# Expert products of layer 0 with tokens on partitions, gated results summed into the residual

## The chip, the cores and the metric

One core of a Trainium2 chip runs the whole program in one launch. The metric is device microseconds of one execution, as the median of several runs; lower is better. The engines are PE (TensorE: matmuls and, beside them, weight loads), DVE (VectorE), ACT (ScalarE), POOL (GpSimd) and SP (SyncE, which here only issues DMAs). They run at their own pace and wait for each other by semaphores.

## The reference, cut to what matters

Two transformer layers over 4096 tokens (16 blocks of 256) of 128 features. The change touches the end of layer 0's attention part and layer 0's expert part:

```
x  = x0
x1 = x + attn(LN(x)) @ w_out + b_out
m  = gelu(LN2(x1) @ w1 + b1) @ w2 + b2                  # 128 -> 512 -> 128
xa = layernorm(x + (x1 + m))
logits = xa @ gate_weight.T                             # [4096, 8]
kth    = sort(all logits)[4*128*6 - 1]
gates  = logits * (logits >= kth)
y_e    = gelu_tanh(xa @ w1_e.T + b1_e) @ w2_e.T + b2_e  # for each of 8 experts
x      = layernorm(xa + sum_e gates[:, e] * y_e)
```

All tokens go through all eight experts (dense). Layer 1, attention and routed experts, follows and is not changed.

## The kernel before, in words

The program runs three stages one after the other: `attention_0` (layer 0's attention), `dense_0` (the m product and the experts of layer 0) and `attention_1` with the routed experts of layer 1. Nothing of one stage overlaps the next: a block ends with all engines.

**attention_0** works on 16 blocks of 256 tokens, pipelined over six stages by a table written by hand (PARTS_0, L150): each engine runs through the same list of parts and does its own share of each. POOL does in "norm" the sum `xs = x + b_out` (L306 to L309), in "stats" the power of -0.5 of the variances, and in "weights" the causal mask (L316). DVE does in "output" `x1 = product + xs` and `xs = x1 + x` (L456, L458). Small inputs come in at the start on ACT's DMA queue (L324); several engines wait for all six of them.

**dense_0** takes chunks of 512 tokens. A *job* is one chunk through one hidden layer: 8 M jobs (the m product, s = 0 to 7) and then 64 pairs (chunk, expert), chunk by chunk. JOBS is 72. All engines run a loop over steps s, and a step does the parts of several jobs, in the order in which they are written in each engine's function:

- PE: `hidden(s+2)`, the up product: 4 blocks of 128 hidden units, each 3 matmuls of 512 tokens (L1045 to L1047). Values and weights are split into a high and a low f16 half, hence three. Then the transposes for M jobs, `down(s)` (L1060), the gate logits, and one small matmul of the search. `down` has the weights stationary and the hidden values moving: 12 matmuls of 512 columns, so its result YB has features on partitions and tokens along the row. YB has two banks.
- ACT: `hidden`: the gelu of each block (L808) and the f16 high half (L813).
- DVE: `low`: the f16 low half (L867), in two passes a job.

After an **M job** ACT evicts YB to accm with scale and bias (L828), PE transposes accm back to tokens on partitions (L1091), DVE adds the residual xs (L982, "post"), does the statistics (L986, L990), POOL the power (L781, L782), and DVE the normalization into xa (L1021). PE turns xa (L1098) for the logits and the pairs. In steps 4 to 11 DVE also makes the low half of one expert's weights (L1030).

**The search** for the kth logit runs on DVE and PE in steps 10 to 27 (COUNT_0 = 10): 15 rounds with three candidates each. Then the gates are known: PE transposes them, DVE copies them to gT (L962), SP stores them to DRAM and broadcasts, for each pair, one gate row of 512 tokens over 128 partitions into the ring G of 6 (L757 to L765).

**Folding.** Until step FOLD_0 = 31 gates are missing, so the results of the first 22 pairs are kept raw: DVE adds the bias and copies YB into buffers that are free by then (L968; x1, xs, hn, h2, stage). From step 31 on each step folds the pair that has just ended (L924: (YB + b2) * G into tmp, L935: acc += tmp), and in 22 of the steps 31 to 68 one kept pair too (L921, L935). When a chunk has all eight experts, PE transposes acc (`turned_sum`, L1078), and the same post adds xa, normalizes and writes xa. Chunks end in steps 41, 44, 49, 57, 59, 65, 69 and 73. In step CLOSING = 69 DVE's order differs, to end early.

Of the kernel before, what the change touches and what calls it, by code (L numbers as in the profile page):

```python
# [87 lines left out]
class Mem:  # L88
# [33 lines left out]
    "d32": (F32, (("b1", ((E + 1) * FB,)), ("cols", (4,)), ("b2", (E,)), ("bitf", (15,)), ("bits", (45,)))),  # L122
# [51 lines left out]
def attention_0(nc, d, keep, rows, stages):  # L174
# [3 lines left out]
    with ExitStack() as ctx:  # L178
# [7 lines left out]
        bo = m.sb("bo", [P, P])  # L186
# [37 lines left out]
        xb_done = m.sem("xb_done")  # L224
# [26 lines left out]
        LOADS, CLEARS = 6, 5  # L251
# [30 lines left out]
        def _(pool):  # L282
# [19 lines left out]
            def step(what, n, k):  # L302
                if what == "stats" and n:
                    power(n)
                if what == "norm":
# [3 lines left out]
                    ins.then_inc(xb_done, 1)  # L309
                if what == "weights":  # L310
# [63 lines left out]
        def _(dve):  # L374
# [3 lines left out]
            def step(what, n, k):  # L378
# [204 lines left out]
COUNT_0 = M_JOBS + 2  # L583
ROUNDS = 15
FOLD_0 = COUNT_0 + ROUNDS + 6
G_RING = 6
LEAD = 2
BEGIN, END = -LEAD - 3, JOBS + 3
CLOSING = JOBS - 1 - LEAD


def job(s):

    return ("m", s, 0) if s < M_JOBS else ("e", (s - M_JOBS) // E, (s - M_JOBS) % E)


def is_pair(s):
    return M_JOBS <= s < JOBS


def kept_raw(s):
    return is_pair(s) and s + 1 < FOLD_0


def raw_pair(s):

    for j in range(M_JOBS, FOLD_0):
        if kept_raw(j) and FOLD_0 + (j - M_JOBS) * 9 // 5 == s:
            return j
    return None  # L610


def folds_0():

    out = []
    for s in range(FOLD_0, JOBS + 1):
        out += [(s, s - 1)]
        if raw_pair(s) is not None:
            out += [(s, raw_pair(s))]
    return out  # L620


def places_0():

    order = [j for _, j in folds_0()]
    chunk = lambda j: job(j)[1]
    place = {j: k for k, j in enumerate(order)}
    opens = {j for k, j in enumerate(order) if all(chunk(i) != chunk(j) for i in order[:k])}
    closes = {j: s for k, (s, j) in enumerate(folds_0()) if all(chunk(i) != chunk(j) for i in order[k + 1:])}
    ended = {s + 1: chunk(j) for j, s in closes.items()}  # L630
    return place, opens, set(closes), ended


def uses_0(ended):

    left, right = [], []
    for s in range(BEGIN, END):
        if 0 <= s - 1 < M_JOBS:
            left.append(("post", s - 1))
        if s in ended:  # L640
            left.append(("epost", ended[s]))
        if 0 <= s - 2 < M_JOBS:
            right.append(("turn", s - 2))
            left.append(("logits", s - 2))
# [1662 lines left out]
def layout(a):  # L2307
# [51 lines left out]
    for t in range(4):  # L2359
        b2[t, :, t] = a["L1_ffn_b2"]  # L2360
# [21 lines left out]
```

## Time and profile before

| | |
|---|---|
| median of 3 runs | 1062.15 us (1059.59, 1062.15, 1066.69) |
| span of the profiled execution, first to last instruction | 1062.5 us |
| attention_0 | 0 to 244 us |
| dense_0: M jobs; pairs | 244 to 350 us; 350 to 691 us |
| attention_1 and routed experts | 692 to 1062 us |
| PE, DVE, ACT, POOL busy | 944.1, 859.6, 756.3, 405.7 us |

The profiled execution has no time of its own beside its span, which stands 0.35 us above the median. How to read rows: engines' times are in us from the first instruction; a line number such as L924 is that of the kernel. In the order of time a row is: start, length, engine, line, operation, written tile <- read tiles, shape, count, and in brackets how long the engine sat idle before it and what ended that. PEld are weight loads, SPq and ACTq the queues that issue DMAs. Matmuls are pipelined, so the length of one is longer than the distance from one start to the next, and the distance counts.

### The profile page before, as it was taken

Reading aid. Unit: us, or ns where it says so; the run is one execution under the profiler, and the core shown is the slowest. Engines: PE = TensorE matmul, PEld = TensorE weight load, DVE = VectorE, ACT = ScalarE, POOL = GpSimd, SP = SyncE. Lnnn points to the kernel's source line nnn. Section 1 sums busy time; section 2 is a strip of 40 time slices with the busy share of each in tenths; the row PEclk is TensorE's granted clock in tenths of the full one; section 3 lists DMA queues with packets and bytes.
Section 4 is the critical chain, followed back from the end, with each engine's and each line's share of the span. In section 5 each row is a group of like instructions: output and inputs, shape, how many; then the busy total and the mean of one; then the engine's idle time right before and its main releaser. Section 6 shows DMA issues by size and latency. Waiting matters only on the chain. (4 is left out here: it accounts for less than half of the span.)

```text
span 1062.5 us, 28952 instructions
## 1 busy us (share of the span) xinstructions
PE 944.1 (89%) x10222; PEld 607.5 (57%) x10222; DVE 859.6 (81%) x2328; ACT 756.3 (71%) x1476; POOL 405.7 (38%) x568
## 2 busy tenths in 40 slices
PE   5999999994889999999999999678888874899996
PEld 3788888872445444444444444246666653788862
DVE  4988988845888999868899999848888866888854
ACT  2666666645889888888888878346767653688854
POOL 3544444443354100000000000023478867676653
PEclk9999999967899999999999999969999985999998
DMA  8333333000002200032212222010111102232318
GB/s 268 123 107 107 107 106 108 24 3 20 1 6 74 72 1 1 1 104 70 77 71 75 87 66 74 20 53 22 32 52 51 54 27 74 75 86 82 85 45 221
DMA packets 61005, 72.60 MB, mean 68 GB/s; under 512 B 8875, under 2 KB 37805, under 8 KB 60865
## 3 DMA queue, kind: packets, MB, share of 16 engines
q1 hardware_dynamic: 50080, 59.36, 17.9%
q0 software_dynamic: 4544, 8.60, 2.4%
q10 hardware_dynamic: 6240, 2.79, 1.1%
q8 instruction: 86, 1.41, 0.6%
q14 instruction: 55, 0.44, 0.2%
HBM read 40.14 MB, written 31.49 MB: 67 GB/s over the span
## 5 line engine op out<-in xcount | busy, mean ns | idle before, releaser
L808 ACT ACTIVATE d__hf<-d__HB,dense__d 128x512 f32<-128x512 f32 x288 | 184.7, 679 | 39.2 <-PE d__HB L1047 38.2
L867 DVE TENSOR_TENSOR d__hl<-d__hf,d__hh 128x1024 f16<-128x1024 f32 x144 | 173.6, 1219 | 20.4 <-ACT d__hh L813 18.1
L813 ACT ACTIVATE d__hh<-d__hf 128x1024 f16<-128x1024 f32 x144 | 152.2, 1057 | 4.6
L781 POOL TENSOR_SCALAR d__rstd<-d__mv 128x4 f32<-128x4 f32 x16 | 14.2, 886 | 353.6 <-DVE d__mv L990 353.6
L1045 PE MATMUL d__YB<-d__hh,d__w2h 128*128 128x512 f16 x288 | 110.5, 384 | 2.5 <-DVE d__tmp L924 2.5
L1046 PE MATMUL d__HB<-d__xl,d__w1h 128*128 128x512 f16 x288 | 110.9, 385 | 0.0
L1045 PE MATMUL d__HB<-d__xh,d__w1h 128*128 128x512 f16 x288 | 110.8, 385 | 0.0
L1047 PE MATMUL d__HB<-d__xh,d__w1l 128*128 128x512 f16 x288 | 110.6, 384 | 0.0
L316 POOL TENSOR_SCALAR_AFFINE_SELECT a__pt<-a__pt 128x512 f32<-128x512 f32 x128 | 81.3, 657 | 75.4 <-ACT a__pt L364 75.3
L1046 PE MATMUL d__YB<-d__hl,d__w2h 128*128 128x512 f16 x288 | 110.1, 382 | 0.0
L1047 PE MATMUL d__YB<-d__hh,d__w2l 128*128 128x512 f16 x288 | 109.9, 382 | 0.0
L423 DVE TENSOR_REDUCE a__mx<-a__S 128x4 f32<-128x512 f32 x128 | 82.2, 683 | 17.9 <-PE a__S L526 17.7
L1306 POOL DMA_INDIRECT parts<-c__ys,c__dest x78 | 81.0, 1038 | 39.2 <-issue 16.8
L364 ACT ACTIVATE a__pt<-a__ST 128x512 f32<-128x512 f32 x128 | 69.4, 596 | 13.9 <-PE a__ST L542 13.8
L1792 POOL DMA_INDIRECT rows<-b__xr,b__slot x64 | 63.7, 995 | 21.5 <-issue 17.0
L1324 ACT ACTIVATE c__hf<-b__SS,c__bias 128x256 f32<-128x256 f32 x156 | 61.0, 474 | 7.3 <-PE b__SS L1533 6.2
L1460 DVE TENSOR_TENSOR c__hl<-c__hf,c__hh 128x512 f16<-128x512 f32 x78 | 54.2, 695 | 2.7
L1045 PEld LDWEIGHTS d__YB<-d__hh,d__w2h 128*128 128x128 f16 x288 | 28.4, 99 | 36.4 <-DVE d__tmp L924 4.4
L1047 PEld LDWEIGHTS d__HB<-d__xh,d__w1l 128*128 128x128 f16 x288 | 28.5, 99 | 35.1 <-issue 1.9
L1047 PEld LDWEIGHTS d__YB<-d__hh,d__w2l 128*128 128x128 f16 x288 | 28.4, 99 | 34.8 <-issue 1.4
L1045 PEld LDWEIGHTS d__HB<-d__xh,d__w1h 128*128 128x128 f16 x288 | 30.4, 106 | 31.3 <-issue 1.4
L1046 PEld LDWEIGHTS d__YB<-d__hl,d__w2h 128*128 128x128 f16 x288 | 28.4, 99 | 32.4 <-issue 0.8
(402 smaller groups left out, 2544.4 us busy)
## 6 DMA issues: line engine op xcount, KB each, us to landing
rows<-a__blank SPq DMA_DIRECT2D x72, 268.0 KB, 3.2
d__G<-gates SPq DMA_DIRECT2D x64, 256.0 KB, 3.2
c__xin<-rows SPq DMA_DIRECT2D x39, 134.0 KB, 2.2
dense__stage<-e_w SPq DMA_DIRECT2D x16, 256.0 KB, 3.1
b__stage<-e_w SPq DMA_DIRECT2D x32, 128.0 KB, 2.2
c__yb<-parts SPq DMA_DIRECT2D x8, 256.0 KB, 8.4
c__yb<-parts ACTq DMA_DIRECT2D x8, 256.0 KB, 8.9
out<-c__xo SPq DMA_DIRECT2D x8, 256.0 KB, 2.3
```

What stands on the lines that cost most here:

```text
L316: pool.affine_select(out=v, in_=v, compare_op=ALU.is_ge, fill=0.0, base=BK, pattern=[[0, 8], [1, BK]], channel_multiplier=-1).then_inc(cau ...
L364: act.activation(pt[:, u % 4, :], ST[:, u % 2, :], ACT.Exp, scale=scale).then_inc(exp_done, 1)
L423: dve.tensor_reduce(mx[:, u // 4, :, u % 4], S[:, u % 2, :].rearrange("p (a j) -> p a j", a=4), AX.X, ALU.max).then_inc(s_free, 1)
L808: act.activation(hf[:, q, f], HB[:, f], gelu, scale=1.0 / WS, bias=b1[:, at:at + 1]).then_inc(s_["h_free"], 1)
L813: act.activation(hh[:, j % (LEAD + 1), f - 1:f + 1], hf[:, q, f - 1:f + 1], ACT.Copy).then_inc(s_["hi_done"], 1)
L867: dve.tensor_tensor(hl[:, p, f], hf[:, q, f], hh[:, p, f], ALU.subtract).then_inc(s_["lo%d_done" % i], 1)
L1045: pe.matmul(dst, wh, vh, start=begin, stop=False)
L1046: pe.matmul(dst, wh, vl, start=False, stop=False)
L1047: return pe.matmul(dst, wl, vh, start=False, stop=end)
L1306: pool.indirect_dma_start(parts, bass.IndirectOffsetOnAxis(dest[b % RING][:, a:a + 1], 0), ys[b % RING][:, a, :], None, bounds_check=2 * T ...
L1324: ins = act.activation(hf[b % 2][:, f], HB[:, b % 2, f // 2, f % 2], ACT.Gelu, scale=1.0 / WS, bias=bias[:, f, b:b + 1])
L1792: pool.indirect_dma_start(rows, bass.IndirectOffsetOnAxis(slot[n % SENT][:, k, a:a + 1], 0), words[n % SENT][:, a, :], None, bounds_check= ...
```

## The change

1. `down` has the hidden values stationary and the weights moving: 4 token tiles x 4 hidden blocks x 3 = 48 matmuls of 128 columns. YB then has tokens on partitions, and one semaphore y_free, counted over all jobs, replaces yf0 and yf1.
2. An M job's result goes from YB straight into the residual add on DVE; ACT's eviction accm and PE's transposes of it go. The bias b2 of m is added to x by POOL in attention_0 (part "shift" of the first half), from a broadcast mb2 that comes in at the start.
3. The gates stay in SBUF with tokens on partitions. A fold is four instructions of 128x128, xa += gate * y, gate a per-partition scalar. acc, tmp, G, the store and the 64 broadcast loads go.
4. The experts' bias, weighed by the gates, is one 32x512 matmul a chunk, from gT and a b2 laid out for it (d32 grows from 8 to 512 columns for it), issued one step before the chunk's end.
5. FOLD_0 is 28, 19 pairs are kept, and steps 28 to 46 fold one kept pair each. Chunks end in steps 36, 41, 44, 47, 49, 57, 65 and 73. The order of the jobs is the same (M_AT = 0 to 7).

```diff
@@ attention_0
+                if what == "shift" and k == 0:
+                    pool.wait_ge(hn_done, n + 1)
+                    pool.wait_ge(xb_done, n + 1)
+                    for a in range(2):
+                        ins = pool.tensor_tensor(x[:, 2 * n + a, :], x[:, 2 * n + a, :], mb2[:], ALU.add)
+                    ins.then_inc(xm_done, 1)
...
-                             (bo[:], d["b_out"].to_broadcast([P, C])),
+                             (bo[:], d["b_out"].to_broadcast([P, C])), (mb2[:], d["m_b2"].to_broadcast([P, C])),
...
-                    dve.wait_ge(xb_done, n + 1)
+                    dve.wait_ge(xm_done, n + 1)
@@ dense_0, sync
-            sp.wait_ge(s_["gt_done"], 1)
-            cells = gates.rearrange("e (t j) -> (e t) j", j=P).rearrange("(a p) j -> p a j", p=P)
-            sp.dma_start(cells, gT[:]).then_inc(s_["sent"], 16)
-            sp.wait_ge(s_["sent"], 16)
-            for k, j in enumerate(order):
-                _, c, e = job(j)
-                wait(sp, s_["g_used"], k - G_RING + 1)
-                sp.dma_start(G[:, k % G_RING], gates[e:e + 1, toks(c)].to_broadcast([P, CT])
-                             ).then_inc(s_["g_in%d" % (k % G_RING)], 16)
@@ dense_0, scalar
-                c = s - 1
-                if 0 <= c < M_JOBS:
-                    act.wait_ge(s_["y_full"], c + 1)
-                    wait(act, s_["pb_full"], left[("post", c - 2)] + 1 if c >= 2 else 0)
-                    act.activation(accm[:, c % 2], YB[:, c % 2], ACT.Identity, scale=1.0 / WS,
-                                   bias=cols[:, 2:3]).then_inc(s_["yf%d" % (c % 2)], 1)
@@ dense_0, vector
+                    own.link(dve.scalar_tensor_tensor(out=gt[:], in0=L, scalar=kth[:], in1=L, op0=ALU.is_ge,
+                                                      op1=ALU.mult))
+                    dve.tensor_scalar(gates[:], gt[:], 1.0 / WS, None, ALU.mult).then_inc(s_["counted"], 1)
+
+            def weighed(y, j):
+                _, c, e = JOB[j]
+                for a in range(4):
+                    t = 4 * c + a
+                    ins = dve.scalar_tensor_tensor(out=xa[:, t, :], in0=y[:, a, :],
+                                                   scalar=gates[:, t * E + e:t * E + e + 1], in1=xa[:, t, :],
+                                                   op0=ALU.mult, op1=ALU.add)
+                return ins
+
             def fold(j):
...
+                dve.wait_ge(s_["counted"], ROUNDS + 3)
+                dve.wait_ge(s_["y_full"], j + 1)
+                dve.wait_ge(s_["y_free"], j)
+                sums.wait()
+                y = YB[:, j % 2].rearrange("p (a c) -> p a c", a=4)
+                weighed(y, j).then_inc(s_["y_free"], 1)
+
+            def fold_kept(j, evacuated):
+                dve.wait_ge(s_["counted"], ROUNDS + 3)
+                dve.wait_ge(s_["y_free"], evacuated)
+                sums.wait()
+                sums.inc(weighed(raw(j), j))
...
+                    dve.tensor_copy(raw(s - 1), YB[:, (s - 1) % 2].rearrange("p (a c) -> p a c", a=4)
+                                    ).then_inc(s_["y_free"], 1)
...
+                    if s in ended:
+                        c = ended[s]
+                        left_full(dve, "epost", c)
+                        dve.wait_ge(s_["y_free"], min(s, JOBS))
+                        sums.wait()
+                        dve.tensor_tensor(r[:], PB[:].rearrange("p (a c) -> p a c", a=4), xa[:, tiles(c), :],
+                                          ALU.add).then_inc(s_["pb_free"], 1)
+                        dve.wait_ge(s_["pb_free"], left[("epost", c)] + 1)
+                    else:
+                        c = m_at(s - 1)
+                        dve.wait_ge(s_["y_full"], s)
+                        dve.scalar_tensor_tensor(out=r[:], in0=YB[:, (s - 1) % 2].rearrange("p (a c) -> p a c", a=4),
+                                                 scalar=1.0 / WS, in1=xs[:, tiles(c), :], op0=ALU.mult,
+                                                 op1=ALU.add).then_inc(s_["y_free"], 1)
+                        dve.wait_ge(s_["y_free"], s)
@@ dense_0, tensor
             def down(j):
...
+                q, p = j % 2, j % (LEAD + 1)
+                wait(pe, s_["y_free"], j - 1)
+                for half_of in range(2):
+                    pe.wait_ge(s_["lo%d_done" % half_of], j + 1)
+                    for a in range(4):
+                        dst, t = YB[:, q, a * P:(a + 1) * P], slice(a * P, (a + 1) * P)
+                        for f in (2 * half_of, 2 * half_of + 1):
+                            at = (weights_of(j) * FB + f) * P
+                            cut = slice(at, at + P)
+                            pe.matmul(dst, hh[:, p, f, t], w2h[:, cut], start=(a == 0 and f == 0), stop=False,
+                                      skip_group_check=True)
+                            pe.matmul(dst, hh[:, p, f, t], w2l[:, cut], start=False, stop=False,
+                                      skip_group_check=True)
+                            ins = pe.matmul(dst, hl[:, p, f, t], w2h[:, cut], start=False, stop=(f == FB - 1),
+                                            skip_group_check=True)
                 ins.then_inc(s_["y_full"], 1)
...
-                if s in ended and s != CLOSING:
-                    turned_sum(s)
+                if s + 1 in ended:
+                    c = ended[s + 1]
+                    pe.wait_ge(s_["pb_free"], left[("epost", c)])
+                    pe.wait_ge(s_["b2_done"], 1)
+                    part = slice(32 * (c % 4), 32 * (c % 4) + 32)
+                    pe.matmul(PB[:], gT[part, c // 4], b2[part, :], start=True, stop=True).then_inc(s_["pb_full"], 1)
```

## Rows read from the trace of the kernel before

**Rows 1.** The page's span and its busy time (share, instructions).

```profile
span 1062.5 us, 28952 instructions
PE 944.1 (89%) x10222; PEld 607.5 (57%) x10222; DVE 859.6 (81%) x2328; ACT 756.3 (71%) x1476; POOL 405.7 (38%) x568
```

**Rows 2.** By stretch: length; busy PE, PEld, DVE, ACT, POOL; clock, DMA share, GB/s.

```profile
445.00:682.00 237.00, 231.66 (x1084) 106.00 (x1082) 205.90 (x300) 197.91 (x258) 12.10 (x12) 1.00 0.23 72
271.00:366.00 95.00, 82.91 (x437) 45.33 (x435) 83.04 (x208) 82.54 (x121) 39.65 (x36) 0.96 0.13 43
...
40.00:230.00 190.00, 185.39 (x4452) 152.71 (x4442) 164.73 (x394) 125.69 (x249) 93.52 (x164) 0.98 0.25 86
```

**Rows 3.** Order of time on PE, pair stage: one down product and what follows.

```profile
430.99 0.38 PE L1045 MATMUL d__YB<-d__hh,d__w2h 128*128 128x512 f16 x1
...
433.58 0.28 PE L1120 MATMUL d__PB<-d__cnt,d__ones 128*128 128x3 f32 x2
```

**Rows 4.** PE's longest waits, 366 to 690 us: total us, times, longest.

```profile
PE d__PB L1075 <- DVE d__acc L935: 6.0, 3, 3.4
PE d__YB L1045 <- DVE d__tmp L924: 2.5, 3, 1.1
```

**Rows 5.** Order of time on DVE, M stage: one step.

```profile
325.44 0.68 DVE L982 TENSOR_TENSOR d__r<-d__PB,dense__xs 128x512 f32<-128x512 f32 x1
...
330.69 1.95 DVE L1021 TENSOR_SCALAR keep__xa<-d__r,d__mv,d__rstd 128x128 f32<-128x128 f32 x4 [0.51 <-POOL d__rstd L782]
...
333.76 0.68 DVE L982 TENSOR_TENSOR d__r<-d__PB,dense__xs 128x512 f32<-128x512 f32 x1
```

**Rows 6.** Routed layer on PE: order of time, down product; then its weight load.

```profile
944.71 0.22 PE L1545 MATMUL b__BD<-routed__w2h,c__hh 128*128 x1
...
945.99 0.22 PE L1547 MATMUL b__BD<-routed__w2h,c__hl 128*128 x1
946.23 0.28 PE L1531 MATMUL b__SS<-c__xt,routed__w1h 128*128 128x256 f16 x1
...
L1545 PEld LDWEIGHTS b__BD<-routed__w2h,c__hh x152: 95/98/98, 909.9 to 1024.8; 128*128 128x128 f16 x152
```

**Rows 7.** Order of time on PE: transposes of a finished sum; routed bias product.

```profile
519.68 0.60 PE L1075 MATMUL d__PB<-keep__ident,d__acc 128*128 128x128 f32 x4
...
1027.91 1.12 PE L1612 MATMUL b__BA<-c__b,c__gts 32*128 32x512 f32 x2
```

**Rows 8.** Order of time, end of the pair stage (PE and DVE).

```profile
681.38 0.38 PE L1047 MATMUL d__YB<-d__hh,d__w2l 128*128 128x512 f16 x1
...
686.28 0.69 DVE L982 TENSOR_TENSOR d__r<-d__PB,keep__xa 128x512 f32<-128x512 f32 x1
...
689.91 1.11 DVE L1021 TENSOR_SCALAR keep__xa<-d__r,d__mv,d__rstd 128x128 f32<-128x128 f32 x4 [1.51 <-POOL d__rstd L782]
```

**Rows 9.** Order of time: folds, bank's reuse, chunk's end; chain: routed layer's scalar-tensor-tensor.

```profile
492.70 0.74 DVE L924 SCALAR_TENSOR_TENSOR d__tmp<-d__YB,d__b2s,d__G 128x512 f32<-128x512 f32 x1
494.55 1.23 DVE L867 TENSOR_TENSOR d__hl<-d__hf,d__hh 128x1024 f16<-128x1024 f32 x1 [0.27 <-ACT d__hh L813]
495.69 0.68 DVE L921 TENSOR_TENSOR d__tmp<-dense__x,d__G 128x512 f32<-128x512 f32 x1
...
498.96 0.38 PE L1045 MATMUL d__YB<-d__hh,d__w2h 128*128 128x512 f16 x1
...
520.32 0.69 DVE L982 TENSOR_TENSOR d__r<-d__PB,keep__xa 128x512 f32<-128x512 f32 x1 [0.57 <-PE d__PB L1075]
...
525.76 0.69 DVE L921 TENSOR_TENSOR d__tmp<-dense__x,d__G 128x512 f32<-128x512 f32 x1
...
706.59 0.54 DVE b__ctxn L1963 x2
```

**Rows 10.** Attention: POOL's present add (group); a load at the start.

```profile
L308 POOL TENSOR_TENSOR dense__xs<-a__x,a__bo 128x128 f32<-128x128 f32 x32 | 13.8, 451 | 0.1
...
2.62 0.45 ACTq L327 DMA_DIRECT2D a__bo<-b_out  x1
```

More of the change, by code:

```diff
@@ L589, with jobs_0, m_at, ended_0 @@
 CLOSING = JOBS - 1 - LEAD
-def job(s):
-    return ("m", s, 0) if s < M_JOBS else ("e", (s - M_JOBS) // E, (s - M_JOBS) % E)
+M_AT = (0, 1, 2, 3, 4, 5, 6, 7)
+def jobs_0():
+    pairs = ((c, e) for c in range(NC_) for e in range(E))
+    return [("m", M_AT.index(s), 0) if s in M_AT else ("e",) + next(pairs) for s in range(JOBS)]
+JOB = jobs_0()
+COUNT_0 = M_AT[-1] + 3
+KNOWN_0 = COUNT_0 + ROUNDS + 2
+FOLD_0 = KNOWN_0 + 1
+KEPT = [s for s in range(FOLD_0 - 1) if JOB[s][0] == "e"]
+FIRST_OF = [JOB.index(("e", 0, e)) for e in range(E)]
+def m_at(s):
+    return JOB[s][1] if 0 <= s < JOBS and JOB[s][0] == "m" else None
 def is_pair(s):
-    return M_JOBS <= s < JOBS
-def kept_raw(s):
-    return is_pair(s) and s + 1 < FOLD_0
+    return 0 <= s < JOBS and JOB[s][0] == "e"
 def raw_pair(s):
[L607 to L615, printed above, removed]
+    i = s - FOLD_0
+    return KEPT[i] if 0 <= i < len(KEPT) else None
+def ended_0():
+    last = {}
     for s in range(FOLD_0, JOBS + 1):
-        out += [(s, s - 1)]
+        if is_pair(s - 1):
+            last[JOB[s - 1][1]] = s
         if raw_pair(s) is not None:
[L619 to L631, printed above, removed]
+            last[JOB[raw_pair(s)][1]] = s
+    return {s + 1: c for c, s in last.items()}
 def uses_0(ended):
@@ L637, in uses_0, with dense_0 @@
     for s in range(BEGIN, END):
[L638 to L644, printed above, removed]
-        if 0 <= s + LEAD + 2 < M_JOBS:
-            right.append(("lift", s + LEAD + 2))
+        if s + 1 in ended:
+            left.append(("epost", ended[s + 1]))
+        if m_at(s - 2) is not None:
+            right.append(("turn", m_at(s - 2)))
+            left.append(("logits", m_at(s - 2)))
+        if m_at(s + LEAD + 2) is not None:
+            right.append(("lift", m_at(s + LEAD + 2)))
         if 0 <= s - COUNT_0 <= ROUNDS + 1:
             left.append(("sum", s - COUNT_0))
-        if s == COUNT_0 + ROUNDS + 2:
+        if s == KNOWN_0:
             left.append(("gates", 0))
     return {u: k for k, u in enumerate(left)}, {u: k for k, u in enumerate(right)}
-def dense_0(nc, d, keep, gates, rows, stages):
+def dense_0(nc, d, keep, stages):
     with ExitStack() as ctx:
@@ L1100, in _ @@
                     down(s)
-                if s in ended and s == CLOSING:
-                    turned_sum(s)
-                if 0 <= c < M_JOBS:
+                if c is not None:
                     wait(pe, s_["pb_free"], left[("logits", c)])
@@ L2327, in layout, with per_tile @@
     down = lambda w: np.ascontiguousarray(w.reshape(-1, FB, P, C).transpose(2, 0, 1, 3).reshape(P, -1))
+    def per_tile(b):
+        z = np.zeros((4, E, 4, C), np.float32)
+        for t in range(4):
+            z[t, :, t] = b
+        return np.tile(z.reshape(4 * E, 4 * C), (4, 1))
     per_row = lambda b: np.ascontiguousarray(b.reshape(-1, P).T)
@@ L2357, in layout @@
     out["c32"] = pack("c32", c)
-    b2 = np.zeros((4, E, 4, C), np.float32)
-    for t in range(4):
-        b2[t, :, t] = a["L1_ffn_b2"]
-    out["e1_b2"] = np.tile(b2.reshape(4 * E, 4 * C), (4, 1))
+    out["e1_b2"] = per_tile(a["L1_ffn_b2"])
     out["gate0"] = np.ascontiguousarray(a["L0_ffn_gate_weight"].T)
```

184 lines of the change are left out of this document (56 added, 128 removed).

## The prediction

> **What bounds the kernel now.** I read the page first: a span of 1062.5 us, with PE marked busy for 89% of it [rows 1]. That figure is an average over stages, so the second view was the busy time by stretch. Layer 0's attention (40 to 230 us) has PE busy 185 of 190 us. The eight M jobs (271 to 366 us) have PE, DVE and ACT each at about 83 of 95 us, so there a loop of waits sets the pace. From 445 to 682 us, where the expert pairs run, PE is busy 231.7 of 237 us at a granted clock of 1.00, and DVE only 206 [rows 2].
>
> A busy PE may still not be a PE at its peak, so the third view was the order of time on PE. In the pair stage a down product starts at 430.99 us and the next PE work at 433.58: 12 matmuls of 512 columns in 2.59 us, 0.216 us each, with no gap [rows 3]. With the 12 of the up product a step is 5.18 us. So **from about 366 us on** the stage is PE's issue of columns. Its waits there are few: 6.0 us in three places for the chunk's finished sum, the longest 3.4, behind the last down, and 2.5 us in three for a result bank [rows 4]. From 366 us to the last down's end at 681.76 [rows 8], less 5.1 us of stalls, at 5.2 us a step: 59 down products.
>
> In the M stage one step lasts 8.32 us: from the residual add at 325.44 to the next at 333.76. In it DVE waits for POOL's 1/sqrt at 330.69; the add itself waits for nothing [rows 5]. The loop is add, statistics, POOL, normalization, weight split, next add. ScalarE's eviction and PE's four transposes are not in it.
>
> **The change, part by part.**
>
> *Down product with tokens on partitions.* The same columns are issued as 48 matmuls of 128 columns, each with its own weight load. The routed layer already does this: 24 such matmuls start between 944.71 and 945.99 us, 23 intervals of 0.0557 us [rows 6]. 48 of them are 2.67 us against 2.59: +0.08 us a step, 59 steps, **+4.7 us**. The 13 steps before hide it under DVE's loop. Below: 0, the same column rate as now. Above: the routed block's next matmul starts 0.24 us after the last one, 0.18 more than the pitch; that on every step would be +10.6.
>
> *The Trainium skill, TensorE: Matmul & The Clock Gate, The mechanism,* says that a weight load overlaps running matmuls only where their row groups differ, which would put 48 full-height loads in series. The load lasts 98 ns here [rows 6], and 24 load-matmul pairs took 56 ns each, so this trace disagrees with the rule; it is kept as a rival of small weight.
>
> *Bias by a matmul instead of a per-partition add.* Each chunk ends with a 32x512 f32 product. The routed layer's equal one spans 1.12 us; the four transposes that it replaces span 0.60 [rows 7]. Both lengths hold one pipelined end, so the difference is what PE loses: 0.52. Seven of the eight lie in the PE-bound stretch: 7 x 0.52 = **+3.6 us**. The eighth stands after the last down, beside DVE's last fold. Bounds: 0, if it overlaps its neighbours as f16 matmuls do, and 7 x 1.12 = 7.8, if nothing overlaps.
>
> *PE's stalls.* The transposes of the finished sum go, and with them PE's wait for it; the bias product needs only the gates and a free bank, one step earlier. Two of the three waits lie before the last down: 6.0 - 3.4 (the tail's) = 2.6 us [rows 4]. The 2.5 us for the result bank come where DVE carries a second fold and a chunk end in the last steps; the second folds are over by step 46 and no chunk ends in step 69. **-5.1 us**, at worst -2.6.
>
> *The tail.* The last down's last matmul starts at 681.38 and the last normalization, begun at 689.91, takes 1.11: 9.3 us after the down's end at 681.76. In it DVE is held by a chunk end, then two folds of two instructions, PE's transposes, and the closing norm of 4.74 us (686.28 to 691.02) [rows 8]. Afterwards one fold (1.08, below) with 0.2 us of semaphores is left before the same 4.74: 6.0 us, **-3.2**.
>
> *Folds on DVE.* A fold is two 512-wide instructions now, 1.58 us from 492.70 to the next low pass at 494.55 less its 0.27 idle. It becomes four of 128x128 with a pointer scalar. The nearest row is the 96-wide one of the same form from PSUM: two in 0.54, 0.27 each, so 1.08 a fold [rows 9]. That gain alone buys nothing: DVE isn't the bound there. But the second folds move from 22 spread over steps 31 to 68 to 19 in a row, steps 28 to 46, and chunks end in steps 36, 41, 44, 47, 49, 57, 65 and 73. A double step is 2 x 1.14 (low pass, 494.55 to 495.69) + 2.16 = 4.4 us against PE's 5.26, so DVE gains 0.8 on PE. A chunk end costs DVE 5.44 less one low pass = 4.3 (520.32 to 525.76) and PE 0.5, so it falls 2.9 behind. Step 36: 2.9; 41: 2.9 again; 44: 4.2; 47 (single fold): 4.4; 49: 4.4. The slack is the time between a fold's end (492.70 + 1.08) and the down that reuses its bank at 498.96: 5.2 us [rows 9]. The lag stays inside: **0**. The price if not is a rival below.
>
> *M stage.* The residual add becomes a scalar-tensor-tensor: 0.74 us instead of 0.68 (rows 9 and 5), eight times, **+0.5**. ScalarE's eviction and PE's transposes leave, outside the loop: 0. The bank is now freed by this add, a DVE instruction, so the next down but one waits for DVE; but PE's turn of the normalized rows, queued ahead of that down, waits for a later DVE instruction of the same step already. Above: nothing more. Below: -12 us, all that PE's waits in this stretch hold (95 less 83).
>
> *Gates.* The 64 broadcast loads and one store on SP go. No wait of PE names them, so 0. The added gate scaling is one 128x256 DVE instruction: under 0.5 us, inside DVE's slack.
>
> *Attention.* POOL gets two 128x128 adds for each of 16 blocks, like the present ones of 0.451 us [rows 10]: 14.4 us, on an engine busy 93.5 of 190 us. They are queued ahead of the mask of the next weights, whose idle time covers them; DVE's new wait is three stages later. The cost that is left is DVE: its four-instruction normalization takes 1.95 us where POOL works beside it (330.69) and 1.11 where POOL is idle (689.91) [rows 5, 8]. DVE has 25 us free of 190, and PE only 4.6 [rows 2]. I take **+1.0**, between 0 and 14.4. *The Trainium skill, SBUF — State Buffer, SBUF: two separate sides,* calls this an exclusive lock: one engine fully blocks the other. If DVE were blocked for every added add and had no slack, the sum would be 14.4 in place of 1.0; the trace agrees that POOL slows DVE, but shows 25 us of slack on DVE.
>
> *Start.* One load more stands on ScalarE's queue ahead of a wait that holds PE's first scores; the one before it took 0.45 us to issue [rows 10]. **+0.3**, 0 to 0.45.
>
> *Sum:* 4.7 + 3.6 - 5.1 - 3.2 + 0 + 0.5 + 1.0 + 0.3 = +1.8. 1062.5 + 1.8 = 1064.3. The profiled execution's span stands 0.35 us above the median of the timed runs (1062.15), so against that median the forecast is 1064.
>
> **The rivals.**
>
> *Faster.* The M stage runs at the pace of its engines, not of its loop: 12 us less; ACT and PE, both relieved, would have had to set it. With the bias hidden (-3.6) and no loss in attention (-1): 1064 - 16.6 = 1047. For it: all three engines are equally busy there. Against it: the add waits for nothing, and DVE's wait is for POOL.
>
> *Slower, by DVE's lag.* If the four small instructions cost 0.375 us each, a fold is 1.5 us, a double step equals PE's, and nothing is won back between chunk ends: 3.65, 7.3, 10.9, 13.1, 13.8 us behind by step 49, less 5.2 of slack: 8.6 us of PE stall between steps 41 and 49. 1064 + 8.6 = 1073. It decides from about 1.3 us a fold. For it: the row has 96 columns and two instructions; four of 128 that read PSUM and add into the same tile are not in this trace. Against it: nothing in the shape suggests a third more.
>
> *Slower, by gaps.* Each down ends with 0.18 us before the next matmul, as in the routed block: 59 x 0.18 = 10.6: 1075. Against it: the routed block reads a register there.
>
> *Weight loads in series.* 48 x 0.098 = 4.70 instead of 2.67: 59 x 2.03 = 120 us, 1184. Against it: the 24 pairs of the routed block. This is what the rule quoted above from the Trainium skill (TensorE: Matmul & The Clock Gate, The mechanism) would give.
>
> **How the numbers follow.** One per cent is 10.6 us, about what a measurement of this kernel can tell from no change: 1051.5 to 1072.8. Forecast 0.62 (its own range: 1059, with bias, attention, start and add at 0, to 1071, with stalls of 2.5 left and the bias at 7.8), faster rival 0.10, lag 0.13, gaps 0.13, series 0.02. So faster 0.10, same 0.62, slower 0.28. The range reaches down to 1055, half way to the faster rival, and up to 1077, past the lag and the gaps.
>
> **What would show it.** Down matmuls at 0.056 us pitch with PE full from about 366 us; no wait of PE for DVE in the pair stage; a tail of about 6 us; M steps still of 8.3 us; the bias product near 1 us. PE waiting for a fold between steps 41 and 49 would show the lag; gaps after each down the other. M steps well below 8 us, or attention longer by more than 5 us, would make the forecast wrong.

## The result, and the profile after

| | before | after |
|---|---|---|
| median of 20 runs each | 1063.47 us (1059.57 to 1066.69) | 1068.08 us (1063.09 to 1073.05) |
| ratio to before, 95% interval | | 1.0049 (1.0033 to 1.0066) |
| span of the profiled execution | 1062.5 us | 1068.2 us |

The change is slower by 4.6 us, half a per cent: clear of the noise, but inside the one per cent that the forecast called no change. The forecast's sum was +1.8. The page of the kernel after answers to [rows 1]: PE 7 us busier, DVE 16 us less, and a fifth more instructions, nearly all of them on PE.

```profile
span 1068.2 us, 34167 instructions
...
PE 951.2 (89%) x12766; PEld 711.0 (67%) x12766; DVE 843.2 (79%) x2462; ACT 751.6 (70%) x1468; POOL 419.5 (39%) x600
```

The busy time by stretch after the change, columns as in [rows 2]:

```profile
40.00:230.00 190.00, 185.47 (x4464) 152.37 (x4466) 164.24 (x395) 126.01 (x250) 104.08 (x190) 0.98 0.24 86
271.00:366.00 95.00, 79.06 (x830) 60.17 (x829) 80.64 (x206) 75.70 (x111) 39.23 (x35) 0.96 0.15 43
445.00:682.00 237.00, 237.00 (x2631) 169.35 (x2630) 190.91 (x432) 199.81 (x261) 13.84 (x14) 1.00 0.01 2
```

In the pair stage PE is now busy for all 237 us; it no longer waits for DVE, and yet the stage is not shorter. In the M stage PE, DVE and ACT all have less to do in the same time: a loop of waits sets the pace there still. In attention POOL does 10.6 us more, and DVE's time hardly moves.

The order of time on PE after the change, answering to [rows 3, 7 and 8]: a down product of the search stage (48 matmuls), the sum behind it and the next up product; a chunk's bias product and the down product behind it; the last matmul of the last down.

```profile
434.25 0.22 PE L1051 MATMUL d__YB<-d__w2h,d__hh 128*128 128x128 f16 x1
...
436.93 0.34 PE L1097 MATMUL d__PB<-d__cnt,d__ones 128*128 128x3 f32 x2
437.12 0.38 PE L1026 MATMUL d__HB<-d__xh,d__w1h 128*128 128x512 f16 x1
...
492.81 0.38 PE L1028 MATMUL d__HB<-d__xh,d__w1l 128*128 128x512 f16 x1
493.12 1.12 PE L1072 MATMUL d__PB<-dense__d,d__gT 32*128 32x512 f32 x2
494.17 0.23 PE L1051 MATMUL d__YB<-d__w2h,d__hh 128*128 128x128 f16 x1
...
688.28 0.22 PE L1055 MATMUL d__YB<-d__w2h,d__hl 128*128 128x128 f16 x1
```

The down product takes 434.25 to 436.93, 2.68 us, 0.0558 a matmul. The sum of the search then takes 0.19 us of PE, where it took 0.14 before. The bias product keeps PE from 493.03 (the matmul at 492.81 and its 0.216) to 494.17, 1.14 us, and nothing overlaps it.

The order of time on DVE after the change: one step of the M stage [rows 5], then the last folds and the end of the stage [rows 8, 9].

```profile
325.31 0.67 DVE L962 SCALAR_TENSOR_TENSOR d__r<-d__YB,dense__xs 128x512 f32<-128x512 f32 x1
...
330.56 1.94 DVE L1002 TENSOR_SCALAR keep__xa<-d__r,d__mv,d__rstd 128x128 f32<-128x128 f32 x4 [0.60 <-POOL d__rstd L765]
...
333.63 0.68 DVE L962 SCALAR_TENSOR_TENSOR d__r<-d__YB,dense__xs 128x512 f32<-128x512 f32 x1
...
688.60 1.12 DVE L896 SCALAR_TENSOR_TENSOR keep__xa<-d__YB,d__gates,keep__xa 128x128 f32<-128x128 f32 x4 [1.55 <-PE d__YB L1055]
689.92 0.69 DVE L956 TENSOR_TENSOR d__r<-d__PB,keep__xa 128x512 f32<-128x512 f32 x1 [0.20 <-DVE keep__xa L896]
...
693.56 1.11 DVE L1002 TENSOR_SCALAR keep__xa<-d__r,d__mv,d__rstd 128x128 f32<-128x128 f32 x4 [1.51 <-POOL d__rstd L765]
```

The M step is 8.32 us as before. A fold is 1.12 us. From the last down's end (688.50) to the end of the last normalization it is 6.2 us instead of 9.3.

**Where the time went.** Marks read off PE's order of time cut both executions into the same pieces. Step s begins with its up product; "lift" is the first transpose of the dense layer.

| piece | before | after | difference | in the prediction's sum |
|---|---|---|---|---|
| first query-key product of attention to the lift | 231.69 | 230.88 | -0.8 | +1.3 (with the start) |
| lift to step 11 (M jobs) | 109.85 | 110.51 | +0.7 | +0.5 |
| step 11 | 5.32 | 6.65 | +1.3 | +0.1 |
| steps 12 to 27 (search) | 85.82 | 88.14 | +2.3 | +1.3 |
| step 28 to the end of the last down | 232.01 | 234.96 | +2.9 | +1.9 |
| from there to the next layer's first product | 10.98 | 7.48 | -3.5 | -3.2 |
| the next layer, code unchanged | 365.76 | 368.21 | +2.5 | 0 |

With 0.3 from the start these make the 5.7 us between the two spans. The dense layer proper, lift to next layer, is 443.98 before and 447.74 after: **+3.8**. The last row, which ends with ScalarE's last instruction, is not the change: over the thirteen kernels of this study that piece is 363.6 to 370.2 us in one profile each, with code that none of them touches (the shortest at a granted clock of 0.94, the longest at 0.91).

### The profile page after: what moved, and what is told of

Read it like the earlier page. It is cut to its first block and busy times, and to the rows that moved or that the text cites. A ratio compares the mean times of both kernels' runs of the same rounds, so it can differ in the third digit from the quotient of the medians.

```text
span 1068.2 us, 34167 instructions
## 1 busy us (share of the span) xinstructions
PE 951.2 (89%) x12766; PEld 711.0 (67%) x12766; DVE 843.2 (79%) x2462; ACT 751.6 (70%) x1468; POOL 419.5 (39%) x600
## 5 line engine op out<-in xcount | busy, mean ns | idle before, releaser
L1051 PE MATMUL d__YB<-d__w2h,d__hh 128*128 128x128 f16 x1152 | 198.3, 220 | 0.0
L1053 PE MATMUL d__YB<-d__w2l,d__hh 128*128 128x128 f16 x1152 | 198.2, 220 | 0.0
L1055 PE MATMUL d__YB<-d__w2h,d__hl 128*128 128x128 f16 x1152 | 198.2, 220 | 0.0
L1051 PEld LDWEIGHTS d__YB<-d__w2h,d__hh 128*128 128x128 f16 x1152 | 113.4, 98 | 12.0 <-issue 5.6
L1053 PEld LDWEIGHTS d__YB<-d__w2l,d__hh 128*128 128x128 f16 x1152 | 113.4, 98 | 6.7 <-issue 0.2
L1055 PEld LDWEIGHTS d__YB<-d__w2h,d__hl 128*128 128x128 f16 x1152 | 113.3, 98 | 0.0
L1283 POOL DMA_INDIRECT parts<-c__ys,c__dest x78 | 81.1, 1039 | 40.0 <-issue 16.5
L896 DVE SCALAR_TENSOR_TENSOR keep__xa<-d__YB,d__gates,keep__xa 128x128 f32<-128x128 f32 x180 | 50.3, 341 | 2.0 <-PE d__YB L1055 2.0
```

The costliest lines, as they stand in the source:

```text
L1051: pe.matmul(dst, hh[:, p, f, t], w2h[:, cut], start=(a == 0 and f == 0), stop=False, skip_group_check=True)
L1053: pe.matmul(dst, hh[:, p, f, t], w2l[:, cut], start=False, stop=False, skip_group_check=True)
L1055: ins = pe.matmul(dst, hl[:, p, f, t], w2h[:, cut], start=False, stop=(f == FB - 1), skip_group_check=True)
L1283: pool.indirect_dma_start(parts, bass.IndirectOffsetOnAxis(dest[b % RING][:, a:a + 1], 0), ys[b % RING][:, a, :], None, bounds_check=2 * T ...
```

## The experiments

The dense layer is the same to some tenths of a us in every kernel that does not change it, so it judges better than the whole time, though it comes from one profile of each kernel. Each ratio is to runs of the kernel before taken beside that kernel (their medians were 1063.0, 1064.4 and 1063.8 us in the three rounds), so the column of medians does not give it. no_bias, narrow_down and wide_m leave out a part of the result or compute on a transposed block; they serve for the time alone.

| kernel | median us | ratio (95%) | lift to next layer | step 11 |
|---|---|---|---|---|
| before | 1063.5 | | 443.98 | 5.32 |
| after | 1068.1 | 1.0049 (1.0033 to 1.0066) | 447.74 | 6.65 |
| no_bias | 1062.0 | 0.9996 (0.9977 to 1.0014) | 440.75 | 6.82 |
| narrow_down | 1067.9 | 1.0033 (1.0011 to 1.0054) | 450.02 | 5.59 |
| late_folds | 1068.9 | 1.0046 (1.0025 to 1.0067) | 447.95 | 6.82 |
| pool_adds | 1080.6 | 1.0164 (1.0131 to 1.0196) | 448.27 | 6.83 |
| act_evict | 1066.4 | 1.0031 (1.0006 to 1.0056) | 447.63 | 6.61 |
| split_first | 1065.5 | 0.9998 (0.9980 to 1.0016) | 444.85 | 5.46 |
| bias16 | 1060.8 | 0.9968 (0.9953 to 0.9983) | 442.24 | 6.83 |
| early_load | 1067.1 | 1.0030 (1.0011 to 1.0048) | 445.47 | 5.46 |
| all_three | 1059.1 | 0.9957 (0.9941 to 0.9973) | 439.33 | 5.46 |
| spaced | 1058.8 | 0.9957 (0.9935 to 0.9979) | 438.47 | 5.46 |
| wide_m | 1066.1 (one run) | | 445.72 | 5.46 |

**no_bias: what the bias product costs.**

```diff
...
-                    pe.matmul(PB[:], gT[part, c // 4], b2[part, :], start=True, stop=True).then_inc(s_["pb_full"], 1)
...
-                        dve.tensor_tensor(r[:], PB[:].rearrange("p (a c) -> p a c", a=4), xa[:, tiles(c), :],
-                                          ALU.add).then_inc(s_["pb_free"], 1)
+                        sums.link(dve.tensor_tensor(r[:], x1[:, tiles(c), :], xa[:, tiles(c), :], ALU.max))
```

> The changed kernel without the product of gates and biases that ends each chunk; the experts' second bias is left out of the first layer, and the add at a chunk's end reads a finished tile of SBUF in place of the bank. Theory 1 (PE pays the whole product): in the changed kernel a step with a chunk end lasts 6.43 us on PE where the others last 5.27, so 1.16 us goes seven times, 8.1 us less than the changed kernel, about 1060; the steps with a chunk end last 5.27. Theory 2 (DVE takes its place): a chunk end costs DVE 4.3 us, PE then waits for a result bank, and at most half of it is won, about 1064, with waits of PE for DVE in the pair stage.

The seven steps fell from 6.43 to 5.27 us, but 1.3 us came back, nearly all of it in two other steps, which grew to 5.95 and 5.83. The view of PE's waits (us in total, times, longest) from 445 to 600 us names DVE:

```profile
PE d__YB L1046 <- DVE keep__xa L894: 0.9, 2, 0.5
```

6.8 us went from step 28 to step 69, 7.0 from the dense layer. Theory 1, with a sixth given back as theory 2 has it: the bias product had also been hiding a backlog of DVE.

**narrow_down: the down product alone, in the kernel before.**

```diff
-                for f in range(FB):
...
-                    ins = split_product(YB[:, q], w2h[:, cut], w2l[:, cut], hh[:, p, f], hl[:, p, f], f == 0,
-                                        f == FB - 1)
+                for half_of in range(2):
...
+                    for a in range(4):
...
+                            pe.matmul(dst, hh[:, p, f, t], w2h[:, cut], start=(a == 0 and f == 0), stop=False,
+                                      skip_group_check=True)
...
```

> The kernel before with its down product issued as the changed kernel issues it, 48 matmuls of 128 columns into the same bank; what follows is as before and so works on a transposed block, with the same instructions. Theory 1 (a price on every PE-bound step): 0.09 us on each of 59 steps and 0.05 on each of 16 sums of the search, 6 us more than the kernel before, about 1069.5. Theory 2 (PE's waits for DVE give way): the kernel before waits 5.1 us for DVE in these steps, and a PE that needs 0.09 us more a step lets DVE catch up, so that 2 to 4 us of the 6 are given back, about 1066.

PE's waits from 445 to 690 us in this kernel, against [rows 4]:

```profile
PE d__YB L1071 <- DVE d__tmp L924: 1.4, 2, 1.0
PE d__PB L1081 <- DVE d__acc L935: 1.1, 2, 0.6
```

The plain steps went from 5.18 to 5.27 and the search steps from 5.32 to 5.46, as theory 1 has it. In the pair stage 5.1 us of waits became 2.5, as theory 2 has it: step 28 to the last down took only 1.3 us more, where 44 downs at 0.09 would be 4.0. So half of the waits that the change removes would have gone through the slower down product alone. The M stage grew by 2.1 us, of which 1.7 is one step in which the logits came late from a PE at the lower clock (308 to 318 us, last section); neither theory had that.

**late_folds: are the early folds what removed the waits?**

```diff
-    i = s - FOLD_0
-    return KEPT[i] if 0 <= i < len(KEPT) else None
+    at = {FOLD_0 + 2 + i * 9 // 5: j for i, j in enumerate(KEPT)}
+    return at.get(s)
```

> The changed kernel with the 19 kept results folded in at steps 30 to 62, nine steps for every five folds as in the kernel before, instead of steps 28 to 46 in a row. Theory 1 (a fold of four small instructions is cheap enough anywhere: 2 x 1.14 + 2 x 1.12 = 4.5 us of DVE in a double step against 5.27 of PE): no wait of PE for DVE in the pair stage and the changed kernel's time within 1 us, about 1068. Theory 2 (the early place removes the waits): PE waits again where second folds and chunk ends meet in steps 48 to 64, 2.5 us or more, about 1071.

Every plain step stays at 5.27 us, no wait of PE is left between 453 and 690 us, and the dense layer differs by 0.2. Theory 1: the early place did not remove the waits, and a fold of 1.12 us (1.58 before) is free anywhere. How the removal divides among the cheaper fold, the transposes that are gone and a slower PE this run does not show; narrow_down gives half of it to the slower down product, and no_bias 1.3 us of waiting to the bias product's cover.

**pool_adds: are POOL's adds hidden, and by what?**

```diff
...
+                    for a in range(6):
+                        pool.tensor_tensor(dead[:, a], bo[:], mb2[:], ALU.add)
```

> The changed kernel with six more 128x128 adds on POOL behind the two new ones of each attention block, into a tile that nobody reads: 96 adds of 0.45 us, 43 us more on POOL. Theory 1 (POOL's adds are hidden, also where DVE works beside them): the attention's end moves by less than 1 us, about 1068. Theory 2 (every add holds DVE up for its length, and the 25 us that DVE has free between 40 and 230 us take the first part): 43 - 25 = 18 us more, about 1086.

Attention grew by 10 us (first query-key product to its last output product 234.1 us; 221.3 to 225.5 in the twelve others). Neither theory. The groups of DVE's longest instruction, after and then here (busy, mean ns, idle before it and by whom):

```profile
L430 DVE TENSOR_REDUCE a__mx<-a__S 128x4 f32<-128x512 f32 x128 | 82.1, 683 | 16.4 <-PE a__S L533 15.9
```

```profile
L433 DVE TENSOR_REDUCE a__mx<-a__S 128x4 f32<-128x512 f32 x128 | 82.4, 686 | 39.3 <-PE a__S L536 39.0
```

And PE's waits in the attention of this kernel:

```profile
PE a__OT L564 <- POOL a__pt L326: 10.2, 14, 1.2
```

DVE was not held up: its reductions are as long as before, and its normalization is no longer either (0.51 us on average, 0.64 after the change). PE waits 14 times for the causal mask that stands behind the adds in POOL's own queue. Two adds a block are covered by POOL's idle time, and eight are not. It is the queue that has a price here, not the neighbour engine.

**act_evict: was ACT's eviction in the M loop?**

```diff
...
+                c = m_at(s - 1)
+                if c is not None:
+                    act.wait_ge(s_["y_full"], c + 1)
+                    act.activation(dead[:, c % 2], x1[:, tiles(c), :].rearrange("p a c -> p (a c)"), ACT.Identity,
+                                   scale=1.0 / WS, bias=cols[:, 2:3])
```

> The changed kernel with a 128x512 activation on ScalarE in each of the eight M steps, at the place where the kernel before evicted the down product, into a tile that nobody reads. Theory 1 (the eviction was not in the loop that sets the M step): the last M steps stay at 8.32 us from residual add to residual add and the changed kernel's time within 1 us, about 1068. Theory 2 (ScalarE sets the pace there): 8 x 0.6 = 5 us more, about 1073.

ACT's order of time shows the added activation between two jobs:

```profile
340.12 0.71 ACT L810 ACTIVATE d__dead<-dense__x,dense__d 128x512 f32<-128x512 f32 x1
```

The dense layer is 0.1 us shorter, not 5 longer. Theory 1 in the whole, though the steps did not stay as it said: the last two came out at 7.7 and 7.9, and the one from 309 us on at 9.5 instead of 8.8. So taking ScalarE's time for the eviction away could win nothing. PE's transposes are not put back here; that they were not in the loop either rests on the M steps of 8.32 us with and without them.

**split_first: what does set the M step?**

```diff
+                if s == BEGIN + 1 or s + LEAD + 2 in FIRST_OF:
+                    j = 0 if s == BEGIN + 1 else FIRST_OF.index(s + LEAD + 2) + 1
...
+                    ins.then_inc(s_["w_done"], 1)
...
                 if post:
...
                     dve.wait_ge(s_["rstd_done"], closed)
...
-                if s == BEGIN + 1 or s + LEAD + 2 in FIRST_OF:
...
-                    ins.then_inc(s_["w_done"], 1)
```

> The changed kernel with DVE's split of the next expert's weights (two instructions, 1.2 us) moved within its step from behind the normalization to ahead of the wait for POOL's 1/sqrt. Theory 1 (the M step is DVE's own loop, with 0.4 to 0.8 us of waiting for POOL in it): the split fills that wait, the steps from 305 us on go from 8.32 to about 7.6 us, 3 us in all, and the stage buffer comes free earlier, so that the step that waits for the last experts' weights (6.65 us instead of 5.46) loses 1.2 us as well: 4 less, about 1064. Theory 2 (the loop goes through PE, which waits 13.4 us for the normalized rows): the rows come 0.5 us later in each step, and the stage is 0 to 3 us longer, 1068 to 1071.

DVE's order of time in one M step of this kernel: the split (L1003) fills the time in which the normalization (L1014) waited for POOL.

```profile
330.74 0.69 DVE L962 SCALAR_TENSOR_TENSOR d__r<-d__YB,dense__xs 128x512 f32<-128x512 f32 x1
...
335.15 0.68 DVE L1003 SCALAR_TENSOR_TENSOR d__w1l<-dense__stage,d__w1h 128x512 f16<-128x512 f32 x1
...
336.35 1.95 DVE L1014 TENSOR_SCALAR keep__xa<-d__r,d__mv,d__rstd 128x128 f32<-128x128 f32 x4
338.34 0.69 DVE L962 SCALAR_TENSOR_TENSOR d__r<-d__YB,dense__xs 128x512 f32<-128x512 f32 x1
```

That step is 7.60 us: the loop is DVE's, as theory 1 has it. But the steps before it were 7.99 and 8.10, since DVE then waits for the logits from PE (5.0 us in the stage instead of 3.8), so the M jobs gave 1.0 us and not 3. The other 1.9 of the 2.9 came from steps 11 and 12, where the weights are now in time.

**bias16: is PE's time the price of the bias, or the wait for its inputs?**

```diff
...
+                    own.link(dve.tensor_copy(gs[:, :, 0], cells))
+                    own.inc(dve.tensor_copy(gs[:, :, 1], cells))
+                    own.link(dve.tensor_tensor(gs[:, :, 2], cells, gs[:, :, 0], ALU.subtract))
...
-                    pe.matmul(PB[:], gT[part, c // 4], b2[part, :], start=True, stop=True).then_inc(s_["pb_full"], 1)
+                    pe.matmul(PB[:], gT[:, c], b2s[:], start=True, stop=True).then_inc(s_["pb_full"], 1)
...
```

> The changed kernel with the gates and biases split into a high and a low f16 part, stacked to 96 rows (high, high, low against high, low, high), so that a chunk's bias is one f16 matmul of 512 columns. Theory 1 (columns on PE are the price): the product goes from 1.16 to 0.22 us, a step with a chunk end from 6.43 to 5.48, 6.6 us in all, less about 1.2 that DVE's chunk ends give back as they did without the product: 5 less than the changed kernel, about 1063. Theory 2 (the wait for gates and bank is the price, not the columns): the step stays near 6.4, about 1068.

PE's order of time at the same chunk's end:

```profile
494.10 0.38 PE L1082 MATMUL d__PB<-d__b2s,d__gT 96*128 96x512 f16 x1
494.32 0.22 PE L1062 MATMUL d__YB<-d__w2h,d__hh 128*128 128x128 f16 x1
```

0.22 us, and a step with a chunk end is 5.49. The dense layer lost 5.5 us; steps 49 and 51 gave 0.8 back, as without the product. Theory 1: PE's time was the price, and not a wait. The columns are 512 in both kernels, so what made the product dear is the f32 format and not their number.

**early_load: why did step 11 grow?** ACT's order of time shows it. After the change, and then in the kernel before:

```profile
355.69 0.63 ACT L802 ACTIVATE d__w1h<-dense__stage 128x512 f16<-128x512 f32 x1 [3.37 <-DMA dense__stage<-e_w]
```

```profile
353.99 0.63 ACT L820 ACTIVATE d__w1h<-dense__stage 128x512 f16<-128x512 f32 x1 [1.40 <-DMA dense__stage<-e_w]
```

The load was issued at 350.4 to 350.5 us in both and landed 5.3 us later after the change, 3.5 before.

```diff
-                sp.wait_ge(s_["w_done"], j - 1)
+                wait(sp, s_["w_done"], j - 2)
...
-                    sp.dma_start(stage[:, j % 2, a], d["e0_" + n][:, (j - 1) * CT:j * CT]
+                    sp.dma_start(stage[:, j % 3, a], d["e0_" + n][:, (j - 1) * CT:j * CT]
...
```

> The changed kernel with a third stage buffer for the experts' weights, so that every load is issued one expert earlier. Theory 1 (a late landing of weights makes the step at 358.75 us last 6.65 us in place of 5.46): the step is 5.46 again and ScalarE waits for no weights, 1.2 us less, about 1067. Theory 2 (ScalarE is late there for another reason, its own order or the wait for PE): the step stays at 6.65.

Step 11 is 5.46 and step 12 too (6.65 and 6.18 before this edit); the dense layer is 2.3 us shorter. Theory 1, and worth more than was expected of it.

**wide_m: why did the load land late?**

```diff
+                for f in range(FB if JOB[j][0] == "m" else 0):
...
+                    ins = split_product(YB[:, q], w2h[:, cut], w2l[:, cut], hh[:, p, f], hl[:, p, f], f == 0,
+                                        f == FB - 1)
-                for half_of in range(2):
+                for half_of in range(2 if JOB[j][0] == "e" else 0):
```

> The changed kernel with the down product of the eight M jobs alone issued as before, 12 matmuls of 512 columns; the add after it works on a transposed block. PE's program is 288 matmuls shorter, so its instruction loads fall elsewhere. Theory 1 (an instruction load on the same DMA engines holds up the last packets of the weights that land at 355.7 us): if no instruction packet falls between that load's issue and its landing, the load lands some 3.4 us after its issue, as in the kernel before, and the step at 358.75 is back at about 5.5 us; if one still falls there, it stays near 6.7. Theory 2 (the late landing has to do with the order of the queues or the places of the tensors): near 6.7 with no instruction packet beside the load.

The DMA view from 350 to 356 us (GB/s in 40 slices of 0.15 us, then the queues' packets, MB and share), after the change and then before it:

```profile
GB/s 0 0 0 0 0 0 0 0 96 68 82 137 355 328 259 246 369 369 382 396 260 178 27 0 0 0 0 14 14 14 0 14 14 27 14 0 0 0 0 55
...
q1 hardware_dynamic: 292, 0.53, 31.2%
q8 instruction: 1, 0.02, 1.0%
q14 instruction: 1, 0.01, 0.7%
```

```profile
GB/s 0 0 0 0 0 0 0 0 0 27 137 177 273 314 177 259 273 301 355 410 410 301 55 27 0 0 0 0 0 0 0 0 0 0 0 0 0 0 0 55
...
q1 hardware_dynamic: 292, 0.53, 28.3%
```

In both kernels nearly all of the load is moved by 353.6 us, but after the change eight packets of 2 KB come one by one until 355.2, at 14 GB/s, as if one of the 16 DMA engines alone were left with them. A q8 instruction packet of 0.02 MB runs from 353.16 to 354.08 us, just ahead of them; before there is none. The same trickle of eight and the same packet stand beside this load in late_folds, act_evict, bias16, no_bias and pool_adds, and beside the next load in early_load. In wide_m the load landed 3.5 us after its issue and step 11 was 5.46:

```profile
353.07 0.63 ACT L802 ACTIVATE d__w1h<-dense__stage 128x512 f16<-128x512 f32 x1 [0.73 <-DMA dense__stage<-e_w]
```

There a q8 packet came too, but only at 353.0 us, after the load's last packets (352.7 us), and none trailed. That is as theory 1 has it, and against theory 2 wide_m has the tensors and queues of the change.

The thirteen traces say more. Of their 182 loads of expert weights behind the two at the start, seven took more than 4.9 us to land, and all others at most 4.1. Beside each of the seven a q8 packet started 2.4 to 2.6 us after the issue, and the first of the eight late packets started within 0.02 us of that packet's end. One more load, in split_first, had a q8 packet as early (2.5 us), when all but its last few packets had moved, and landed in 3.2. In narrow_down a q8 packet lies ahead of the load (351.6 to 352.5 us); nothing trails there, but ACT waits 2.2 us for the weights and step 11 is 5.59, between the two. So the packet holds these eight up as far as times can tell; no run moved the packet and nothing else. That the late landing is the price of steps 11 and 12 is shown by early_load.

**all_three and spaced: a version that beats both.** The edits of split_first, bias16 and early_load together, and then with the kept folds placed apart:

```diff
-    i = s - FOLD_0
-    return KEPT[i] if 0 <= i < len(KEPT) else None
+    at = list(range(FOLD_0, FOLD_0 + 7)) + list(range(FOLD_0 + 8, FOLD_0 + 17)) + [47, 50, 52]
+    return KEPT[at.index(s)] if s in at else None
```

> The changed kernel with the three edits together: DVE's weight split ahead of the wait for POOL, the bias as one f16 product of 96 rows, and a third stage buffer for the weights. Theory 1 (each edit takes its own piece): from the first lift of the dense layer to the next layer's first product the bias took 5.5 us off, the split 2.9, of which 1.9 is the late weights that the third buffer also removes: 8.4 less than the changed kernel's 447.7, 439.3 us, and 4.7 less than the kernel before's 444.0; the whole about 1059.5. Theory 2 (they share a limit, DVE, which then stalls PE): 441 or more, about 1062.

> As the kernel with the three edits, with the kept results folded so that chunks end at steps 36, 40, 44, 48, 52, 56, 64 and 72 instead of 35, 40, 43, 46, 48, 56, 64 and 72. Theory 1 (PE's 1.2 us of waiting for DVE near step 50, which came when the bias product no longer held PE, is DVE's backlog of chunk ends close together): no wait of PE for DVE in the pair stage, 1 us less than with the three edits, about 1058.5. Theory 2 (the waits belong to the folds themselves): they stay, the same time.

The dense layer came to 439.33 us, as added up, and with the spaced folds to 438.47, with no wait of PE for DVE in the pair stage and 5.27 or 5.49 us in every step from 28 on. (The steps that the second expectation lists are those of the bias product, one before the chunk's end.) Theory 1 both times. Both kernels are 0.43% faster than the kernel before, 0.85% faster than the change by the medians; between the two the whole time does not tell.

## Why the prediction was right, and where its size was off

"No change" held, and the rivals fell as weighed: no M stage at the engines' pace (steps of 8.32), no lag of DVE (PE without a wait in the pair stage, a fold of 1.12 us where 1.08 was taken), no gaps (a plain step of 5.27 us is 12 matmuls at 0.216 and 48 at 0.056, with nothing left over) and no weight loads in series. On that last one the rule from the Trainium skill (TensorE: Matmul & The Clock Gate, The mechanism), that a load overlaps matmuls only of other row groups, does not hold here: 48 full-height loads of 98 ns with their matmuls take 2.68 us. In the lag's working a chunk end costs 4.3 less PE's 0.5, which is 3.8 and not 3.65; the rival's price would be 9 us instead of 8.6, and it fell all the same.

Term by term:

- *Down product, +4.7.* Right in kind: +0.09 a step where +0.08 was taken, 5.3 on 59 steps (two more steps, 11 and 12, had PE as their limit: 0.2). narrow_down shows it alone.
- *Bias, +3.6, and stalls, -5.1.* The failed step is reading both lengths as holding "one pipelined end". The next matmul behind the four transposes at 519.68 us [rows 7] shows what they hold:

```profile
520.12 0.38 PE L1045 MATMUL d__YB<-d__hh,d__w2h 128*128 128x512 f16 x1
```

They keep PE 0.44 us (a step of 5.62 against 5.18), not 0.60, and the product 1.16 (6.43 against 5.27), so 7 x 0.72 = 5.0. The waits were worth more than the view says, since it counts from a matmul's modelled end: before, the steps with transposes and waits took 9.1 us over the plain pitch, of which 7 x 0.44 = 3.1 is the transposes, so 6.0 and not 5.1. Together these are -1.0 where the sum had -1.5: two errors that nearly cancel, by luck.

- *Left out: the search's small sum.* It keeps PE 0.05 us longer behind a narrow matmul, 0.8 us over the search.
- *Left out: the weights' landing.* The M stage's loads were not looked at, since no wait of PE named them; ACT had 1.4 us of waiting there already. It costs 1.2 us in step 11 (6.65 against 5.46) and under 0.1 more than before in step 12; the rest of their growth, 0.14 each, is the down product and the sum.
- *Tail, -3.2.* Measured -3.1 to the end of the last normalization, for the reason given, and -3.5 to the next layer's first product.
- *M stage, +0.5, and the eviction, 0.* Measured +0.7, but not where the sum put it: the scalar-tensor-tensor took 0.67 us like the add, so that the 0.74 read for it was too much. 0.3 of it is the step from 308 us on. act_evict shows the zero for ScalarE's part.
- *Attention +1.0 and start +0.3.* Neither is seen: the two attentions without the adds took 225.5 and 223.7 us, ten with two adds 221.3 to 225.2, and the first query-key product starts at 17.1 and 18.0 us without the added load and 16.5 to 18.3 with it. The term rested on DVE's normalization growing longer beside POOL; in attention it took 0.65 us on average before the change and 0.64 after, and 0.33 at its shortest, so what holds it up was there already. On the Trainium skill's exclusive lock (SBUF — State Buffer, SBUF: two separate sides) the reductions that pool_adds shows (683 and 686 ns) say little, since they read PSUM; the normalization's two lengths would fit it, and no run here takes it apart. The 14.4 that it would give for the added adds was far off: eight adds a block cost 10 us, and those by POOL's queue.

The terms as measured (5.3 + 0.2 - 1.0 + 0.8 + 1.2 - 3.5 + 0.7) make 3.7 us; the dense layer came out 3.8 longer, where the sum had 0.5. That the forecast still held owes something to its wide limit of one per cent. The rest of what the two medians differ by, 0.8 us, lies within the spread of the unchanged last layer.

## What to carry to other kernels

Where one engine is issued full, count every instruction that the edit leaves on it by its distance from start to start, not by its length: removing waits there gains no more than the new instructions take, and here a f32 product of 32 rows took all of it. What a product cost on PE here is its columns and its number format, not its rows (f16: 0.22 us for 96 rows and for 128; f32, in the routed layer before: 1.05 us from 1027.91 to 1028.96 for 32 rows, 1.06 from there to 1030.02 for 128), so stacking the high and low parts along the rows makes a f32-like bias cost one f16 matmul. Look at the count in a row too: the f32 product is two matmuls (x2), while f32 transposes of as many columns are one each and kept PE 0.44 us. And a transfer that lands just in time is a term of the sum, even if no wait names it on the engine that sets the pace.

## What the runs showed that was not expected

- One f32 matmul of 32 rows by 512 columns kept PE 1.14 us; a f16 one of 96 rows by 512 columns 0.22, with the split values of the same product in it; f16 ones of 128 rows keep it 0.216.
- A longer program on PE seems to delay another engine's data: 106 packets of q8 instruction loads instead of 86 in the whole run, and where one fell into the middle of a 256 KB load, the load's last eight packets started only at its end and came up to 2.0 us after the others, in seven kernels.
- In step 4 of the M jobs PE comes back from a wait of 5.1 us at a granted clock of 0.50 (the lower level, 1.2 GHz) from 308 to 312 us and 0.90 from 312 to 316 after the change; before, it is 0.57 and 1.00. That step is 8.80 us instead of 8.47, and in narrow_down, at 0.50 and 0.75, 10.16. How busy PE was between 302 and 308 us does not put the three in order (3.8 us before, 1.2 after, 3.1 in narrow_down).
